# Last graph layer: a step's load waits for its own group's landing, and VectorE's six whole-score operations in pieces

## What is computed

```
h = (x @ W).reshape(N, H, C)                       # H = 4, C = 32
row, col = (ei[0], ei[1])
x_i, x_j = h[row], h[col]
e = einsum(x_i, a_i) + einsum(x_j, a_j)
e = leaky_relu(e, negative_slope=0.2)
mask = vmap(topk_mask_1h)(e)                       # the 8 best of each row node, per head
e = where(mask, e, -inf)
seg_max = segment_max(e, row);  ez = exp(e - seg_max[row])
denom = segment_sum(ez, row);   alpha = ez / denom[row]
out = elu(segment_sum(alpha[:, :, None] * x_j, row))
...
x = _layernorm(x + out)
```

## Time and profile before

| | us |
|---|---|
| median of 3 runs | 9274.97 (9267.95 to 9284.56) |
| the profiled execution's own time | 9279.35 |
| its span, first to last instruction | 9277.6 |

### The profile page before, as it was taken

How to read it: one execution, slowest core, us unless ns; L and a number is a source line. 1 busy time by engine, 2 the same in 40 slices (tenths; PEclk the granted TensorE clock), 3 DMA queues, 4 the chain that set the end, 5 groups by cost and what they waited for, 6 DMA issues and landing times. The chain is left out here.

```text
span 9277.6 us, 191808 instructions
## 1 busy us (share of the span) xinstructions
PE 6584.0 (71%) x41828; PEld 5506.0 (59%) x41829; DVE 6344.5 (68%) x11887; ACT 1633.8 (18%) x4649; POOL 6372.1 (69%) x7772
## 2 busy tenths in 40 slices
PE   5999999999278458777777617999678820057643
PEld 3888778788177447666666516777467720046533
DVE  3444444444677867777777417888678899989736
ACT  1111111110221034444444200111500000011000
POOL 2777777774078467777777746888267788887771
PEclk9999999999799789999999759999889965589856
DMA  4777777776067346666666699999179943379864
GB/s 116 207 207 210 207 206 208 207 205 195 11 200 210 100 145 213 208 206 209 209 210 206 212 125 220 269 270 272 43 220 262 261 131 86 86 212 256 220 160 113
DMA packets 2113960, 1742.98 MB, mean 188 GB/s; under 512 B 376688, under 2 KB 1838118, under 8 KB 2113686
## 3 DMA queue, kind: packets, MB, share of 16 engines
q1 hardware_dynamic: 1217548, 819.30, 30.1%
q10 hardware_dynamic: 710140, 472.87, 20.8%
q0 software_dynamic: 186160, 449.72, 17.2%
HBM read 1289.62 MB, written 453.29 MB: 188 GB/s over the span
## 5 line engine op out<-in xcount | busy, mean ns | idle before, releaser
L1591 POOL DMA_INDIRECT z_xg<-table,srci x1664 | 1832.2, 1101 | 511.5 <-issue 475.1
L1162 POOL DMA_INDIRECT sorted<-m_rows,srci x1612 | 1606.2, 996 | 533.1 <-issue 441.3
L464 POOL DMA_INDIRECT g_xg<-table,srci x1612 | 1584.0, 983 | 491.1 <-issue 459.4
L1458 PE MATMUL n_ps<-n_row,n_oh 128*128 128x257 f32 x3712 | 882.4, 389 | 216.7 <-DVE n_row L1434 200.3
L483 PE MATMUL g_psg<-g_wg,g_eT 128*128 128x136 f32 x3224 | 1027.5, 474 | 0.0
L1458 PEld LDWEIGHTS n_ps<-n_row,n_oh 128*128 128x128 f32 x3712 | 677.8, 190 | 421.2 <-issue 339.4
L1651 PE MATMUL z_ps<-z_wrow,z_oh 128*128 128x132 f32 x3712 | 615.5, 317 | 404.4 <-DVE z_wrow L1818 183.2
L500 PE MATMUL g_psx<-scores,g_hot 128*128 x3608 | 835.9, 362 | 70.9 <-DVE e_score L591 69.1
L483 PEld LDWEIGHTS g_psg<-g_wg,g_eT 128*128 128x128 f32 x3224 | 769.3, 324 | 191.0 <-issue 191.0
L500 PEld LDWEIGHTS g_psx<-scores,g_hot 128*128 128x128 f32 x3608 | 806.9, 329 | 86.4 <-issue 84.9
L564 DVE TENSOR_TENSOR g_y<-g_gate,g_xg 128x512 f32<-128x512 f32 x403 | 279.6, 694 | 795.3 <-DMA g_xg<-table,srci 794.0
(11 more groups left out here) (411 smaller groups left out, 12544.4 us busy)
## 6 DMA issues: line engine op xcount, KB each, us to landing
n_row<-sorted SPq DMA_DIRECT2D x464, 520.0 KB, 4.4
z_buf<-gathered ACTq DMA_DIRECT2D x464, 256.0 KB
g_keys<-dst_row ACTq DMA_DIRECT2D x451, 256.0 KB
ag_buf<-gated SPq DMA_DIRECT2D x451, 256.0 KB, 3.2
m_keys<-dst_row ACTq DMA_DIRECT2D x451, 256.0 KB
gathered<-z_xg SPq DMA_DIRECT2D x416, 256.0 KB
gated<-g_y SPq DMA_DIRECT2D x403, 256.0 KB
g_eT<-in_attr_t SPq DMA_DIRECT2D x402, 256.0 KB
```

The source lines that it names most:

```text
L464: nc.gpsimd.indirect_dma_start(out=xg[:, u, j, :], out_offset=None, in_=v.table[:, :], in_offset=bass.IndirectOffsetOnAxis(ap=v.srci[:, t: ...
L1162: nc.gpsimd.indirect_dma_start(out=v.sorted[:, :], out_offset=bass.IndirectOffsetOnAxis(ap=place[:, t:t + 1], axis=0), in_=rows[:, u, j, : ...
L1458: last = nc.tensor.matmul(ps[u % 4][:, 0:ROW], oh[:, u, j, :], row[:, u, j, 0:ROW], start=(j == 0), stop=(j == G - 1))
L1591: nc.gpsimd.indirect_dma_start(out=xg[:, u, j, :], out_offset=None, in_=v.table[:, :], in_offset=bass.IndirectOffsetOnAxis(ap=v.dsti[:, t: ...
```

## The change

It has two parts, both in `stage_last_layer`.

First, SyncE counts the landings. After each store it waits, one group late, for that store to land and adds 1 to a new semaphore `s_land`. ScalarE's wait `stored` is gone; in its place `load` reads the group's number g and waits for `s_land` to reach g + 1, so step k waits for the landing of its own group. The number is read with `value_load`, which keeps the check of the bounds.

Second, each of the six operations over all scores is written as eight, one for each head and half.

```
@@ sync
+                def landed(g, u, use):
+                    sp.wait_ge(s_st[u], use * 16 + 16)
+                    sp.sem_inc(s_land, 1)
+
-                pipeline(sp, GS, (store, 0), ring=U)
+                pipeline(sp, GS, (store, 0), (landed, 1), ring=U)
@@ scalar
-                def stored(k, u, use):
-                    act.wait_ge(s_st[u % U], use * (16 * R // U) + 16 * (u // U + 1))
-
                 def load(k, u, use):
-                    g = step_value(nc, act, steps, 0, k, GS - 1)
+                    g = act.value_load(steps[0:1, 0, ds(k, 1)], min_val=0, max_val=GS - 1)
                     if later(k, R):
                         act.wait_ge(s_w, k - R + 1)
+                    act.wait_ge(s_land, g + 1)
                     act.dma_start(buf[:, u, :, :], out[:, ds(g * G, G), :]).then_inc(s_ld[u], 16)
...
-                pipeline(act, KS, (stored, 0, GS), (load, 0), ring=R)
+                pipeline(act, KS, (load, 0), ring=R)
@@ vector
-                nc.vector.tensor_tensor(VV, VV, seg.behind[:, :, :], ALU.add).then_inc(s_e, 1)
+                bits = [(h, slice(a, z)) for h in range(H) for a, z in seg.cuts]
+                for h, c in bits:
+                    last = nc.vector.tensor_tensor(VV[:, h, c], VV[:, h, c], seg.behind[:, h, c], ALU.add)
+                last.then_inc(s_e, 1)
...
+                for h, c in bits:
+                    last = nc.vector.tensor_scalar(seg.behind[:, h, c], VV[:, h, c], -1.5 * BIG, None, ALU.is_lt)
+                last.then_inc(s_dve, 1)
```

More of the change, by code:

```diff
@@ L1535, in stage_last_layer @@
     s_bt, s_bc = sem("z_bt"), sem("z_bc")
+    s_land = sem("z_land")
     s_z, s_oh, s_w, s_wc, s_mm, s_add = (sem("z_" + n) for n in ("zero", "oh", "w", "wc", "mm", "add"))
@@ L1760, in _ @@
                 dve.wait_ge(s_set, 3)
-                nc.vector.tensor_tensor(VV, VV, seg.behind[:, :, :], ALU.add).then_inc(s_e, 1)
+                bits = [(h, slice(a, z)) for h in range(H) for a, z in seg.cuts]
+                for h, c in bits:
+                    last = nc.vector.tensor_tensor(VV[:, h, c], VV[:, h, c], seg.behind[:, h, c], ALU.add)
+                last.then_inc(s_e, 1)
                 dve.wait_ge(s_e, 1)
-                nc.vector.scalar_tensor_tensor(VV, VV, 0.2, VV, ALU.mult, ALU.max).then_inc(s_e, 1)
+                for h, c in bits:
+                    last = nc.vector.scalar_tensor_tensor(VV[:, h, c], VV[:, h, c], 0.2, VV[:, h, c], ALU.mult, ALU.max)
+                last.then_inc(s_e, 1)
                 for d, r in enumerate((fl.rf, fl.rb)):
@@ L1767, in _ @@
                 fl.rf, fl.rb = flag
-                bits = [(h, slice(a, z)) for h in range(H) for a, z in seg.cuts]
                 def knock_out(it):
@@ L1788, in _ @@
                 seg.dve(dve, 0)
-                nc.vector.tensor_tensor(orig, seg.before[:, :, :], seg.behind[:, :, :], ALU.max).then_inc(s_dve, 1)
+                for h, c in bits:
+                    last = nc.vector.tensor_tensor(orig[:, h, c], seg.before[:, h, c], seg.behind[:, h, c], ALU.max)
+                last.then_inc(s_dve, 1)
                 dve.wait_ge(s_dve, 1)
-                nc.vector.tensor_tensor(orig, VV, orig, ALU.subtract).then_inc(s_dve, 1)
+                for h, c in bits:
+                    last = nc.vector.tensor_tensor(orig[:, h, c], VV[:, h, c], orig[:, h, c], ALU.subtract)
+                last.then_inc(s_dve, 1)
                 dve.wait_ge(s_dve, 2)
@@ L1796, in _ @@
                     knock_out(it)
-                nc.vector.tensor_scalar(seg.behind[:, :, :], VV, -1.5 * BIG, None, ALU.is_lt).then_inc(s_dve, 1)
+                for h, c in bits:
+                    last = nc.vector.tensor_scalar(seg.behind[:, h, c], VV[:, h, c], -1.5 * BIG, None, ALU.is_lt)
+                last.then_inc(s_dve, 1)
                 dve.wait_ge(s_dve, 3)
                 dve.wait_ge(s_exp, 1)
-                nc.vector.tensor_tensor(seg.before[:, :, :], orig, seg.behind[:, :, :], ALU.mult).then_inc(s_dve, 1)
+                for h, c in bits:
+                    last = nc.vector.tensor_tensor(seg.before[:, h, c], orig[:, h, c], seg.behind[:, h, c], ALU.mult)
+                last.then_inc(s_dve, 1)
                 nc.vector.memset(acc[:, :, 0:width], 0.0).then_inc(s_z, 1)
```

## The result

| | before | changed |
|---|---|---|
| median, us | 9271.46 (9266.33 to 9284.56, 4 runs) | 9187.15 (9181.77 to 9190.95, 4 runs) |
| the profiled execution's own time | 9279.35 | 9190.8 |

A forecast was written before the change was run, and what follows sets the result against it. GpSimd's own chain of gathers was taken as the bound, with 49 products behind the last landing. -75.0 + 12.4 - 20.0 = -82.6 us took the profiled 9279.35 to 9196.8, as a median 9192 us; range 9179 to 9213.

The forecast's parts named there:

- Term 1: Tail before the update: each step waits for its own group's landing, so 48 steps leave the tail; -75.0 us.
- The signs named for it: Tail: one to three products behind the last landing, update about 15 us after last gather's start; steps not under 0.5 per us.
- Term 2: Gathers beside the steps: steps moved earlier lengthen the fast stretch and delay gathers; +12.4 us.
- Term 3: ScalarE's loads in the steps: the added bounds check and register operations are covered by VectorE's pace; 0 us.
- Term 4: SyncE's stores: waiting for landings one group late is covered by at least 5 us; 0 us.
- Term 5: Gathers beside the six operations over all scores: cutting these into eight pieces lets more gathers through; -20.0 us (18.5 to 21.4).
- this case as an end of the term: Gathers beside the mask: its pieces block nothing, giving 7.8 us there; pieces' best total -21.4 us.
- The sum: Whole kernel: -75.0 + 12.4 - 20.0 = -82.6 us, giving 9192 us.
- 1: Rival at the six operations: pieces help only at the mask; sum -64.6 us, 9210 us; chance 0.06.
- 2: Rival in the steps: early steps are nearly free for gathers, 2 us instead of 12.4; 9182 us; chance 0.08.
- 4: Rival on SyncE: waiting for landings holds the stores and GpSimd stands; slower, 9375 us; chance 0.03.
- 3: Rival in the steps: ScalarE's longer chain sets the pace, so steps don't get ahead; about 9256 us; chance 0.03.

The follow-up runs named there:

- the two single experiments: Kernel before with only the landing waits (six operations whole): 9214.36 us; kernel before with only the six operations cut (old waits): 9246.72 us.
- the third experiment: Kernel before with the landing waits and, of the six operations, only the mask cut in pieces: 9207.89 us, ratio 0.9921.
- the first: Kernel before with only the landing waits, the six operations left whole: 9214.36 us, ratio 0.9932.

## Why the prediction was right

- **Term 1, -75.0:** the tail from the last gather to the update went from 90.5 to 14.8 us, -75.7. The signs named for it came out: two products behind the last landing, the update 14.8 us behind the last gather's start, no pace lost.
- **Term 2, +12.4:** 14.3 us with the landings alone. In the changed kernel the fast stretch reaches to 8852 us instead of 8830; at the rates of the earlier trace rows 127 us more of it are 11.3 gathers, 14.1 us. The size was right as a difference of two stretches, which is what moved steps change. As a price of one step it was not: 0.275 us was put on the 204 steps above the slack rate, and the weights in PSUM show 0.16 on average over all 464. The same 56 us over all 304 steps of the fast stretch are 0.18. The DMA traffic has no part in it that shows: at a share of 0.95 the gathers take 0.943 us.
- **Term 3, 0:** right here, with 304 steps in 500 us as before. The dearer chain is there (the shortest distances between two loads are 1.27 to 1.36 us, before 0.97 to 1.07), and it is covered. Its cover, 2.01 us a step against 1.64, belongs to the chip: on the slower one 1.98 us were there and 2.17 needed.
- **Term 4, 0:** 28.5 us of waiting on SyncE, none longer than 1.7. Without the lag it would have cost more than half of the gain, some 50 us of 84.
- **Term 5, -20.0:** 22.9 us less from first to last gather with the pieces alone. The part that was mis-sized is the mask: its pieces were charged with 1.87 us a gather and 4.1 us of VectorE, and hold no gather but take 5.08 us. The prediction had this case as an end of the term, at -21.4. The pieces of L1767 and the rest have 1.57 + 0.30 us, the figure of the earlier trace rows.
- **The sum** was -82.6 and the profiled executions differ by 88.5 us, their spans by 88.8. Of these, 75.7 are the tail, 1.4 the first gather's start, and 11.7 lie between first and last gather. There terms 2 and 5 together were put at 7.6, and the two single experiments add up to 8.6. So the two terms together were some 4 us short, and nothing is left for the look-up stage: VectorE's section begins 5.9 us earlier, but the 501st gather starts at 7414.2 us, before at 7413.7. At the 1001st gather, early in the steps, the lead is 23.8 us, at the last one 13.1 instead of the 7.6 forecast (9092 instead of 9098 us). To which of the two terms the 4 us belong isn't shown, since single traces differ by as much (the first gather lies between 6747.7 and 6763.8 us in the kernels of this text on the chips of the 9270 us kind). The medians, 84.3 us apart, are nearer to the sum than the traces are; that much is luck.
- **The rivals:** 1 fell with the third experiment, 2 with the first. 4 did not occur, but the kernel without lag is its small brother: GpSimd held by stores that were held by landings. 3 got 0.03, and its outcome is what happens on the slower chips, though not by its mechanism as far as is shown; the trace of one chip could not show it.

## What to carry to other kernels

Where a wait by turn stands for a wait by data, count in the trace how many steps run behind the last landing; their sum, less what they cost the bounding engine when they run early, is what an exact wait gives. Let the counting engine wait one item late, for a count right behind the issue serialises the transfers. Ask at what pace the freed steps run against the time that is there for them, and hold that margin against more than one chip. Where a chip is slower, compare the sequencers' shortest, median and longest instruction before blaming the kernel.

Where GpSimd issues many gathers beside VectorE, read the gathers' durations beside each kind of VectorE operation: here a second input from SBUF is what they waited for, so try to cut such operations, or to move a small operand to PSUM.

## What the runs showed that was not expected

- The mask (one input) holds a gather for 4.71 us as one operation of 3.63 us, and holds none in eight pieces, which take 5.08 us together: GpSimd gains 7.4 us in the traces for 1.45 on VectorE.
- Pieces of 416 values let a gather follow every 1.50 us (1.20 + 0.30), but beside the 16 pieces of L762 in the segmented scans single gathers took 4.8 to 6.5 us.
- A product with its small operand in PSUM leaves the gathers at 0.94 us; with both in SBUF the same product of 0.68 us makes them 1.16. This was worth 76 us of the gathers' chain (9116 us on one chip, 9187 on another), nearly as much as the change.
- The kernel before takes 9271 to 9280 us on some chips and 10934 and 11012 on two others, with equal durations of the gathers and products, and episodes in which the sequencers' instructions take 0.70 us each. On one of the latter the change costs 0.3% where it gives 0.9% on the former.
